# A graph network on one core: count matrix with a column per node, first pass in loops of three turns

## The reference

```python
def _gin_conv(x, src, dst, W_a, b_a, W_b, b_b):
    agg = jax.ops.segment_sum(x[src], dst, num_segments=N)
    h = agg + x
    h = jax.nn.relu(h @ W_a + b_a)
    return h @ W_b + b_b
...
for _ in range(K):                       # second layer, K = 2
    x = jax.ops.segment_sum(x[src] * norm, dst, num_segments=n)
```

## Time and profile before

| quantity | value |
|---|---|
| time, median of 3 runs | 13891.47 us (13890.89 to 13902.91) |
| span of the profiled execution | 13892.9 us |
| busy PE / DVE / ACT / POOL | 8563.9 / 7277.8 / 2041.8 / 9883.4 us (62 / 52 / 15 / 71%) |
| the chain that ended last | POOL 62%, issue 22%, PE 7%, DVE 4%, ACT 2%, DMA 1% |
| DMA traffic | 930.87 MB in 1111612 packets |

### The profile page before, as it was taken

One profiled execution on the slowest core, in us unless ns is written; L12 is line 12 of the kernel. 1 busy time (PEld: TensorE's weight loads), 2 busy tenths in 40 slices (PEclk: granted clock), 3 DMA queues, 4 the chain that ended last, 5 costly groups with the idle time before them and its releaser, 6 DMA issues.

```text
span 13892.9 us, 190634 instructions
## 1 busy us (share of the span) xinstructions
PE 8563.9 (62%) x45374; PEld 5687.6 (41%) x45374; DVE 7277.8 (52%) x21844; ACT 2041.8 (15%) x1668; POOL 9883.4 (71%) x10259
## 2 busy tenths in 40 slices
PE   5666667776877866666667666667666660033315
PEld 2333323333444445545445545545455540032305
DVE  5555522223333366666666666666666661245637
ACT  5666710000000001111111111111111110000000
POOL 7777747775767757777767777767777765777772
PEclk8887868888989977778878887778778775566657
DMA  4544523344767730000010000010000002122212
GB/s 122 154 143 145 150 70 102 103 107 115 215 181 215 214 75 13 13 13 13 13 16 13 13 13 13 13 16 13 13 13 13 13 12 38 32 57 57 57 39 47
DMA packets 1111612, 930.87 MB, mean 67 GB/s; under 512 B 312738, under 2 KB 1066308, under 8 KB 1111061
## 3 DMA queue, kind: packets, MB, share of 16 engines
q10 hardware_dynamic: 641040, 670.91, 15.8%
q0 software_dynamic: 325632, 190.97, 8.8%
q1 hardware_dynamic: 144518, 64.66, 2.1%
HBM read 718.69 MB, written 207.12 MB: 67 GB/s over the span
## 4 chain that ended last, share of the span: by engine, by line
POOL 62%; issue 22%; PE 7%; DVE 4%; ACT 2%; DVEq 1%; DMA 1%; ACTq 0%; SPq 0%; POOLq 0%
POOL work L802 62%; PE ps L910 2%; PE ps L925 2%; ACT nodes L1289 2%; DVEq L1740 1%; PE ps L1111 1%; PE ps L898 1%; PE ps L1028 0%; DVE big L1750 0%; DVE big L1823 0%; DVE nodes L1762 0%; PE ps L1122 0%; PE ps L1139 0%; DVE nodes L1758 0%; ACTq L1413 0%
## 5 line engine op out<-in xcount | busy, mean ns | idle before, releaser
L802 POOL DMA_INDIRECT work<-tab_sp,nodes x4992 | 4725.1, 947 | 1735.6 <-issue 1520.1
L1006 PE MATMUL ps<-work 128*128 128x192 f32 x9984 | 2671.8, 411 | 1905.9 <-DVE work L1672 1850.4
L1006 PEld LDWEIGHTS ps<-work 128*128 128x128 f32 x9984 | 1992.9, 232 | 2482.0 <-issue 1440.7
L1921 DVE TENSOR_TENSOR work<-work,ps 128x192 f32 x4992 | 1748.3, 350 | 719.9 <-PE ps L1006 372.6
L802 POOL DMA_INDIRECT work<-tab_att,nodes x1664 | 1603.9, 964 | 628.3 <-issue 628.3
L991 PE MATMUL ps<-work,wk 128*32 128x144 f32 x10080 | 1760.9, 327 | 2.3 <-DVE work L1921 2.3
L925 PE MATMUL ps<-nodes,work 128*96 128x480 fp8e4 (+1 forms) x6664 | 1613.9, 400 | 64.7 <-DVEq L1872 59.2
L802 POOL DMA_INDIRECT work<-in_x,idx x1248 | 1302.8, 1044 | 416.8 <-issue 375.5
L1750 DVE TENSOR_TENSOR big<-big,ps 33x12 f32 (+2 forms) x3520 | 554.8, 158 | 1939.5 <-PE ps L898 1214.5
L1672 DVE TENSOR_TENSOR work<-work,ps 128x512 f32<-128x512 f32 x1248 | 856.0, 686 | 1333.5 <-DMA work<-tab_sp,nodes 1317.9
L1331 ACT ACTIVATE work<-zero 128x2496 f32<-128x2496 f32 x318 | 725.4, 2282 | 5453.1 <-PE ps L991 5448.4
(11 more groups left out here) (241 smaller groups left out, 6117.1 us busy)
## 6 DMA issues: line engine op xcount, KB each, us to landing
nodes<-counts_d ACTq DMA_DIRECT2D x612, 660.0 KB
counts_d<-nodes ACTq DMA_DIRECT2D x130, 1188.0 KB
work<-tab_sp,nodes POOLq DMA_INDIRECT x4992, 2.4
work<-counts_d ACTq DMA_DIRECT2D x117, 528.0 KB
work<-edge_rows SPq DMA_DIRECT2D x112, 320.0 KB
edge_rows<-work ACTq DMA_DIRECT2D x104, 320.0 KB, 2.2
work<-tab_att,nodes POOLq DMA_INDIRECT x1664
work<-in_x,idx POOLq DMA_INDIRECT x1248
```

What stands on the lines that cost most here:

```text
L802: pool.indirect_dma_start(out=rows(p, r)[:, t, 0:ROW[p]], out_offset=None, in_=TABLE[p], in_offset=bass.IndirectOffsetOnAxis(ap=place, axi ...
L1006: last = nc.tensor.matmul(moment_place(t), u0[:, s % 2, t % SUB, :], vb[:, t % AHEAD, :, :].rearrange("p k j -> p (k j)"), start=True, sto ...
L1921: v.tensor_tensor(to, to, got, ALU.add).then_inc(mom_added.sem, 1)
```

## The change

**Columns.** A count-matrix column is now a node. Slots are regrouped by destination: a group is the edges into five consecutive nodes (`KN`), padded to 128 slots, 2000 groups in 50 pairs of 40. A group's code has 98 x 5 = 490 columns instead of 1188 and needs one matmul (L945). The evicted result of 40 groups is 200 columns a block, one per node, so sums need no window: DVE adds a unit whole.

**Dense and near parts.** Near halves become 24, 32, 22 and 22. The dense part ends at a node number, not at a tile; at the seam 32 tiles (`CUT`) have slots of both kinds, and `cut_off` shifts their one-hot columns out of range for the pass.

**gin1.** Its dense product reads the evicted counts where they lie in SBUF, one pair behind the building (L958, 98 matmuls of 97x200 a pair); nothing is loaded back. ACT evicts two groups at a time, 980 columns, in code written out, with a ring of three; stores of a pair, 2.53 MB, are SP's. PE and DVE do one turn of 80 groups and then eight iterations of three turns, each with one near half. The list of near sources is loaded once.

**gin2, gcn1, gcn2.** Units are 400 columns (22, 25 and 25 of them), pieces 563 KB with a ring of six, products 128x400 with 64x400, or 96x400 (L1000), one DVE add of 400 columns a unit (L1855). The passes are written out, without loops. Gather rings are four deep for these.

**Setup.** Group boundaries are found by 16 comparisons with accumulated sums; POOL gathers 16 and then 32 small columns of edge numbers; some ten DVE operations of 2048 columns make code and low part; 32 PE transposes and eight ACT copies turn them. The guard compares fourteen pairs instead of ten, and also tests for crowded groups and for seams. The transposes of x lie first on PE.

On PE in gin1, before: one turn's pattern of count matrices (L910), a piece's products (L925) and near sums (L898).

The core of the diff:

```diff
-DENSE = {"gin1": 416, "gin2": 640, "gcn1": DT, "gcn2": DT}
+KN = 5
+KSTEP = 2
+PAIR = 40
+NEAR_HALVES = {"gin1": 24, "gin2": 32, "gcn1": 22, "gcn2": 22}
...
+                for q in range(KSTEP):
+                    hold(pe, "pe", code_made.sem, code_made.done("gin1", n + q))
+                    if q == 0:
+                        pe.wait_ge(evicted.sem, evicted.done("gin1", step - 3))
+                    nc.tensor.matmul(ps[:, 2 * ring + q, 0:KC], lo_oh[:, (b // SUB) % 2, (b + q) % SUB, :],
+                                     code_oh[:, (b + q) % CODE_RING, :], start=True, stop=True).then_inc(built.sem, 1)
...
+                    for t in blocks_:
+                        last = nc.tensor.matmul(ps[0:SPLIT1, 7, 256 * h:256 * h + PN], parts1[:, t, 0:SPLIT1],
+                                                staged_counts[:, h, t * PN:(t + 1) * PN], start=(t == 0),
+                                                stop=(t == NT - 1))
...
+                turn_(0, 0)
+                with pe.Fori(0, near_halves(p) // 3) as i:
+                    for y in range(3):
+                        turn_(3 * i + (1 + y), 1 + y, 3 * i + y, y, i)
...
-                with pe.Fori(0, NEAR_TURNS[p]) as i:
-                    for c, ((u, ch), subs_) in enumerate(steps):
+                for c in range(UNITS[p] * NCH):
+                    (u, ch), r = divmod(c, NCH), c % PIECES
+                    if ch == 0:
+                        hold(pe, "pe", unit_added.sem, unit_added.done(p, u - 4))
...
+                            nc.scalar.activation(out_[:, KSTEP * e:KSTEP * (e + 1), :, :],
+                                                 ps[:, 2 * ring:2 * ring + KSTEP, 0:KC].rearrange("p q (m w) -> p q m w", w=KN),
+                                                 ACT.Copy, saturate=False).then_inc(evicted.sem, 1)
...
+                with sp.Fori(0, PAIRS // 2) as i:
+                    for h in range(2):
+                        j = 2 * i + h
+                        sp.wait_ge(evicted.sem, evicted.done("gin1", STEPS * j + (STEPS - 1)))
...
-                            v.tensor_tensor(window, window, ps[0:m, bank, at_:at_ + LW], ALU.add)\
-                             .then_inc(unit_added.sem, 1)
+                    to = acc[0:m, u * UN:(u + 1) * UN]
+                    v.tensor_tensor(to, to, ps[0:m, u % 4, 0:UN], ALU.add).then_inc(unit_added.sem, 1)
...
+            for c in range(KCOLS):
+                link(v.tensor_scalar(pen_f[:, 0:SEEN], first_target.bitcast(I32)[:, 0:SEEN], group_f[:, c:c + 1], None,
+                                     ALU.is_lt, ALU.add, accum_out=tiles_before[:, c:c + 1]))
```

More of the change, by code:

```diff
@@ L60 @@
 LW = 12
-DT = 1040
-DENSE = {"gin1": 416, "gin2": 640, "gcn1": DT, "gcn2": DT}
[L63 to L68, removed]
-SPLIT1 = 3 * C + 1
[L70 to L74, removed]
+KN = 5
+KSTEP = 2
+PAIR = 40
+PN = PAIR * KN
+PAIRS = 50
+KT = PAIRS * PAIR
+KCOLS = KT // P + 1
+KC = NT * KN
+NCH = 9
+HIS = 11
+ROWB = NCH * HIS * PN
+CHB = HIS * PN
+NEAR_HALVES = {"gin1": 24, "gin2": 32, "gcn1": 22, "gcn2": 22}
+DENSE = {p: ET - G * n for p, n in NEAR_HALVES.items()}
+DENSE_NODES = {"gin1": 9800, "gin2": 8800, "gcn1": PAIRS * PN, "gcn2": PAIRS * PN}
+UNIT = 2
+UN = UNIT * PN
+UNITS = {"gin1": DENSE_NODES["gin1"] // PN, "gin2": DENSE_NODES["gin2"] // UN, "gcn1": DENSE_NODES["gcn1"] // UN,
+         "gcn2": DENSE_NODES["gcn2"] // UN}
+CUT = 32
+SEEN = max(DENSE.values()) + CUT
+PIECES = 6
+CODE_RING = 8
+STEPS = PAIR // KSTEP
+DENSE_FROM = 3
+TURN_K = 2 * PAIR
+NEAR_AT = (2, 12, 22, 32)
+SPLIT1 = 3 * C + 1
 KS = 4
@@ L88 @@
 EPS = 1e-5
-DIST = 10
+DIST = 14
+PAIR_RING = 8
 MOST_CLOSE = 5
-CHECKED = DT * P // ET
+CHECKED = -(-SEEN * P // ET)
+FAR_OFF = 1024.0
 assert ET * P >= E and NT % BT == 0 and BLOCKS % 2 == 0 and ET % P == 0 and HALVES * G == ET
 def ring_of(p, close):
-    return 3 if close and p in ("gin1", "gcn1", "gcn2") else RING
+    return 3 if close and p == "gin1" else RING
 def chunk_halves(q):
@@ L805, in half @@
                         ).then_inc(quarter_in[r][t // SUB] if p in SPLINE else gathered[p][r], 16)
-                if close and p not in ("gin1", "gin2"):
+                if close and p == "gin1":
+                    hold(pool, "pool", near_idx_in, 16)
+                    for k in range(near_halves(p)):
+                        half(k, k % ring, k // ring, near_idx)
+                    return
+                if close and p != "gin2":
                     hold(pool, "pool", all_src_in, 16)
-                    for k in range(near_halves(p) if near else HALVES):
-                        half(k, k % ring, k // ring, True)
+                    for k in range(near_halves(p)):
+                        half(k, k % ring, k // ring, all_src[:, DENSE[p] if near else 0:])
                     return
@@ L1409, in _ @@
             nc.scalar.activation(warm[:, :], work[:, C:C + 1], ACT.Copy)
-            turn("x")
+            act.wait_ge(consts, 9)
+            for b in range(BLOCKS):
+                act.wait_ge(turned_ps.sem, turned_ps.done("x", b))
+                nc.scalar.activation(acc[0:C, b * BN:(b + 1) * BN], flat(2 * (b % 2), BN, C), ACT.Copy).then_inc(turned.sem, 1)
             act.wait_ge(rw_clear, 1)
@@ L1415, in _ @@
                 act.sem_inc(counts_out[h], 16)
+            for q in range(KCOLS // SUB):
+                for part, bank, n in ((code, q, 2 * q + 1), (src_lo, 4 + q, 2 * q + 2)):
+                    act.wait_ge(grid_turned_ps, n)
+                    nc.scalar.activation(part[:, q * SUB * P:(q + 1) * SUB * P], ps[:, bank, :], ACT.Copy).then_inc(grid_turned, 1)
             def rest(close):
                 if close:
-                    store_counts()
+                    evict_counts()
                 else:
@@ L1826, in near_pass, with add_unit @@
+                near_one_hots(p, 0, 0)
+                turn_(0)
+                with dve.Fori(0, near_halves(p) // 3) as i:
+                    for y in range(3):
+                        turn_(3 * i + (1 + y), 3 * i + y, y)
+                add_pair(UNITS[p] - 1, (UNITS[p] - 1) % 2, added.events(p))
             def near_pass(p):
[L1827 to L1830 removed]
+                def add_unit(u, n_added):
+                    m = P if p == "gin2" else 3 * C
```

604 lines of the change are left out of this document (303 added, 301 removed).

## The result

The changed kernel takes 12244.56 us in the median (12242.49 to 12257.91) against 13891.99 us, a ratio of 0.8816 with a 95% interval of 0.8804 to 0.8829. The forecast was 12280 us. The profiled execution spans 12256.2 us, 12 more than the median.

What follows compares the result with a forecast made beforehand. POOL's gathers, issued without a stop, were taken to bound gin1, gin2 and both gcn passes. 13892.9 + 61 (setup) - 549 (gin1) - 485 (gin2) - 2 x 321 (gcn) = 12278, stated as 12280 us, range 12100 to 12700.

Steps and rivals of the forecast that it cites:

- what counts is the longest of the other engines: All four passes: with fewer gathers, each pass lasts as long as its longest engine other than POOL.
- 6 us showing: Setup: of 62 us of POOL's 48 small gathers, all but 6 us lie beside comparisons and guard operations.
- 156 + 70: gin1, DVE: 156 us for 24 turns' near work, plus 70 us (8%) for contention with POOL.
- Rival (b): gin1: evictions into 5-byte runs are slower, total 12750 us at 1.6 us each or 12400 at 1.25; chance 0.11.
- PE's sum of 884: gin1, PE: one-hot products 426 us, dense products 418 and 96 near-sum rounds at 0.42, in all 884 us.
- the extra 182 us: gin1, PE: if weight loads of 0.125 us show whole behind 200 columns, 4802 x 0.038 raises PE to 1066 us.
- 25 us for clock and waits: gcn passes: 25 us in each 488 us sum for a clock of 0.92 and waits on pieces and rows.
- (a): gin1: TensorE runs at 1.2 GHz throughout, the pass takes 1676 us, total 12825 us; chance 0.12.
- (d): All four passes: TensorE at 1.2 GHz makes the kernel slower than before, +346 us, 14240 us; chance 0.02.
- (c): gcn passes: transfers bind at the old 211 GB/s, 635 us each, total 12570 us; chance 0.10.
- (e): Whole program: the stricter guard sends it the wide way, all 1664 tiles of each pass gathered, 17950 us; chance 0.01.
- Straight code costs nothing: Passes written out: they drop their loops' jumps, and straight code adds nothing to the sum.

Runs made afterwards that it cites:

- b1_halfgather: The kernel before the change, with every second gather of gin2 and the gcn passes left out, neighbouring tiles' rows taken instead; 13384.42 us.
- e2_mqw: The changed kernel with evictions walking two groups together, so destination runs are 10 bytes instead of 5; 12132.7 us.
- e8_dve_written: e2_mqw with DVE's gin1 written out instead of in the loop of three turns, PE's still looped; 12070.12 us.
- e7_both: The changed kernel with 10-byte eviction runs, gin1 written out on PE and DVE, and gin2 with 36 near halves; 12019.57 us.
- e5b_halfload: The changed kernel with only one of a piece's two halves loaded in the gcn passes after the first six pieces; 12242.93 us.
- e6_halfproduct: The changed kernel with gcn products taking 200 of a piece's 400 columns, loads and gathers kept; 12224.08 us.
- e3_written: The changed kernel, 5-byte eviction runs kept, with gin1 written out without a loop on both PE and DVE; 12221.38 us.

## Why the prediction was right, and where it was not

**The bound now.** That gathers bound gin2 and the gcn passes was read rightly: POOL has over 70% of the chain there, and POOL is idle between 29 and 67% of each of the four passes now. In gin1 it was half of the matter. The chain of the kernel before in gin1, and the wait of its near sums for gathered rows there:

```profile
by line: issue 17.9%; PE ps L910 17.6%; ACT nodes L1289 12.7%; POOL work L802 12.3%; PE ps L925 10.9%; DVEq L1740 4.8%; PE ps L898 3.7%; DVE big L1823 3.6%; DVE big L1750 3.6%; DVE nodes L1762 3.4%; DVE nodes L1758 2.0%; ACTq L1277 1.1%; DV
...
PE ps L898 <- DMA work<-in_x,idx: 17.9, 6, 9.0
```

POOL gathered almost without a stop all through gin1 (it waited 4.6 us for PE), but PE, ACT and DVE, with the building of the count matrix, were as long: the chain goes over to POOL only near the end, and near sums waited 17.9 us for rows, against 353.6 in gin2. So by this chain the 554 us of gin1 needed the shorter building as well as fewer gathers; how much either gives alone no run shows. That "what counts is the longest of the other engines" held for the new code; for the old one it hides these limits, in gin1 level with the gathers and in gcn 40 us below them (b1_halfgather).

**Setup, +61 and +73.** The comparisons were priced well (1.66 us with the read of the sum, against 1.53). The term that failed is "6 us showing" of the 48 gathers. DVE's timeline in the changed kernel:

```profile
127.75 1.23 DVE L2240 TENSOR_SCALAR nodes<-nodes 128x2048 f32<-128x2048 int32 x1 [22.18 <-DMA nodes<-in_dst_ext,work]
```

The guard's operations end near 105, and DVE stands 22.18 us until the last of 32 gathers has landed; for the first 16 it stood 4.94 us.

**gin1, 1130 and 1125: right by luck, by two errors that cancel.** ACT was taken at 912 us and is 1100: the line through evictions of 896 and 1188 columns says nothing about runs of 5 bytes. With one stretch it measures 0.887, so the columns were priced rightly and the run length is the whole miss. DVE was taken at 1133 us and is some 985 (1015.7 us of gin1 in e2_mqw less 30.9 of waits for PE): one-hots 840 as forecast, jumps 37 instead of 50, adds of 200 columns 17, and so some 90 for near work, contention and the loop's slower succession together, instead of 156 + 70. Written out (e8_dve_written, 915 us) near work and contention are under 60, since adds slip between one-hots and gathers slow them only at times. What the Trainium skill says of small tiles (page "VectorE: DVE Perf Modes", section "The TRN2 errata — SBUF-src ops pay a fixed extra latency per instruction") agrees with this trace: 0.42 us a group is the line's value, not the 0.34 that columns alone would give. Rival (b) is what happened, at 1.10 instead of 1.25 or 1.6 us, and with it a sign that the forecast had named as wrong, evictions above 1.07 us; without its 5-byte runs the kernel would have been at 12133. PE's sum of 884 held (it is busy 903 us in e7_both), as the timeline of the changed kernel shows:

```profile
704.14 0.59 PE L945 MATMUL ps<-nodes 128*128 128x490 bf16 x2
704.57 0.68 PE L958 MATMUL ps<-nodes,work 128*97 128x200 fp8e4 x6
705.11 0.59 PE L945 MATMUL ps<-nodes 128*128 128x490 bf16 x2
```

Two one-hot products hold PE 0.43 us, 0.215 each (forecast 0.213), and six dense ones 0.54, 0.09 each (0.087). So the weight load of 97 columns hides behind 200, and the extra 182 us did not come. An estimated 81 ns from the section "LDWEIGHTS (loading the stationary operand)" of the Trainium skill's page "TensorE: Matmul & The Clock Gate" would hide behind 90 ns too; the trace does not show that price by itself, its loads of 97 columns lasting 125 ns (median) and overlapping.

**gin2, 824 and 831.** The mechanism was right; two terms are off and cancel. PE in gin2 of the changed kernel:

```profile
1814.97 2.03 PE L1000 MATMUL ps<-nodes,work 128*128 128x400 fp8e4 x11
1816.94 2.05 PE L1000 MATMUL ps<-nodes,xc 128*64 128x400 fp8e4 x11
1818.82 0.58 PE L933 MATMUL ps<-work 128*64 128x12 f32 x8
1819.34 2.03 PE L1000 MATMUL ps<-nodes,work 128*128 128x400 fp8e4 x11
```

Eleven products hold PE 1.97 us, 0.179 each instead of 0.174: some 20 us more for 4312. A round of near sums adds 0.43 (forecast 0.42). The 20 us for clock and waits were spent to some 4: the clock was 1.00, and PE waited 1.9 us, before the node phase.

**gcn, 488 and 460.** The mechanism was right and confirmed (e5b_halfload, e6_halfproduct); the allowance for clock and waits was too large. Here is PE within gcn1 and at its end in the changed kernel:

```profile
2505.52 3.92 PE L1000 MATMUL ps<-nodes,work 128*96 128x400 fp8e4 x22
2509.37 0.42 PE L933 MATMUL ps<-work 128*32 128x12 f32 x8
2509.73 5.78 PE L1000 MATMUL ps<-nodes,work 128*96 128x400 fp8e4 x33
2515.44 0.42 PE L933 MATMUL ps<-work 128*32 128x12 f32 x8
...
2831.63 2.66 PE L1184 MATMUL ps<-ident,big 96*128 96x96 f32 x16 [1.85 <-DVE big L1797]
```

22 products hold 3.85 us and 33 hold 5.71, 0.173 to 0.175 each as forecast, 424 to 429 us in all. A round of near sums holds 0.36 from its row's start to the next, not 0.42: 31 us. These make 455 to 460 by themselves, so the 25 us for clock and waits were hardly touched. The tail of 18.41 us is gone as expected: the node phase waits 1.85 us.

**Rivals (a) and (d)**, a PE at 1.2 GHz, had the opposite sign: the granted clock rose in all four passes, in three of which PE stopped waiting between products. (c) did not come; loads are covered even at 0.91 to 0.93 busy. (e) did not come; the close way ran.

**Code.** "Straight code costs nothing" held: e3_written and e7_both are faster than the loops. The term for DVE's jumps, 50 us, was near (36.9); what had no term is the slower succession of DVE's operations inside the loop, 33 us, and the price of PE's loop, some 22 us. Both show only once evictions are shorter (e8_dve_written, e7_both).

## What to carry to other kernels

Price an eviction by the length of its destination's runs as well as by its columns, and let the access pattern walk neighbouring groups together if that doubles the runs. Before crediting a change with removing the bound, ask what is late 5% later: in gcn fewer gathers alone were worth 40 of 349 us. Where several engines are nearly full at once, price a loop on each of them by more than its jumps: here two loops cost 85 us, of which 37 are DVE's stops at the jumps.

## What was not expected of the hardware

ScalarE's evictions of 980 columns from two PSUM banks to fp8 took 1.10 us apart with 5-byte runs, 0.93 with 10-byte runs and 0.887 in one stretch, while one such operation lasted 1.68 us on average with 5-byte runs. Its length is no price: with 10-byte runs the median is 1.06 us in e2_mqw and 1.58 in e7_both, at nearly the same distance. Why short runs cost this was not tried. After a small add of VectorE's (33x12) between one-hots the next operation starts 0.07 to 0.2 us later, in a row of adds 0.24.
